# Mixture-of-experts layer behind gated power attention, one core: the overflow lists, their fetches and the first expert's outputs put elsewhere in the order

## The chip, the cores and the metric

One core of one Trainium2 chip runs the whole kernel as one program. The metric is the device time of one execution in microseconds; less is better. The program has one instruction stream for each engine: TensorE (matmuls and transposes), ScalarE, VectorE, GpSimd (which also issues all indirect transfers) and SyncE (which issues the plain transfers). They meet by semaphores alone, and each stream runs strictly in its order.

## The reference

The input is 4 sequences of 1024 tokens with 256 channels. Two sublayers follow each other, each with a residual and a layer norm behind it:

```python
x = _layernorm(x + attention(x))          # 16 query heads, 8 key heads, gated, squared scores
x = _layernorm(x + ffn(x))

# ffn: N = 4096 tokens, E = 64 experts, TOP_K = 6, F = 176, capacity C = 768 slots of an expert
scores = softmax(x @ gate_w.T); topk_w, topk_idx = top_k(scores, 6)      # weights normalised
buf[e, pos] = x[token]                                                   # the expert's slots
eo = (silu(buf @ w_gate.T) * (buf @ w_up.T)) @ w_down.T                  # for each expert
y[token] += eo[e, pos] * weight
y += shared_swiglu(x)                                                    # FS = 352, for all tokens
```

How many slots of an expert are filled depends on the data: 384 in the mean, at most 768.

## The kernel before

`schedule()` writes one list of tasks by hand, `order`. Each engine's program walks through the whole list and does its own part of every task that it knows. So a task's place in the list is its place in the queue of every engine that has a part in it. There is no planner; waits are written out in each part, and `Once` leaves out a wait that the engine has already passed.

The stages are attention (32 heads), routing (interleaved with the last heads and with the stage behind it), the shared expert, the routed experts, and a last stage that sums two partial outputs and normalises.

The shared expert is done as 16 jobs (`2 * M`, `M = 8` blocks of 512 tokens, two halves of FS each). A job is `gate_up` in 3 parts (TensorE, `gate_up`, L1286), `hidden` in 4 parts (ScalarE L1503 to L1521, VectorE L1892 to L1907), and for each block two `shared_down`. In `shared_up` (inside `schedule`) the steps of the last routing part are mixed in by `paces[k]`, up to job 10.

A routed expert is handled with its first 512 slots (`MAIN`) in a main job. Slots 512 to 767 of experts that have more than 512 tokens are handled by overflow jobs of 256 slots. `KJ = 4` of these have a fixed place in the sequence `SEQ` (places 18, 34, 50 and 67); further ones run in branches at the end. Which expert an overflow job serves is only known at run time: `counted` (L1912) counts the experts with more than 512 tokens and scans the count over the experts, `jobs` (L1927) makes from it, in four chunks of 12, the row numbers of the slots and of the weights. Both run on VectorE, in the buffers `scores` and `onehot` of routing.

For one place of `SEQ` the order is: part 0 of this job's `gate_up`; `turn` of the next job's rows (TensorE transposes 4 tiles in two pairs, `turn_x`; ScalarE makes `xe_hi`, L1530; VectorE makes `xe_lo`, L1969, and picks the token numbers and weights); `split_hi` of the weights two jobs on (ScalarE, L1501) and `split_lo` (VectorE, L1888); parts 1 and 2 of `gate_up`; and the two pairs of `down` of the job *before* (TensorE L863, ScalarE scales them into `y_e`, L1548, GpSimd adds them to `y_part` in DRAM by four indirect transfers of 128 rows each, L2117). `down` and `turn_x` share two PSUM banks in turn: each waits until the use before of its bank has been read (`out_before`). `down` also waits until VectorE has made the lower halves of the job's hidden layer (`c_hl`).

SyncE loads each expert's rows (`rows_in`, L1060) and weights (`raw_in`, L1035); there are four buffers of each. The overflow jobs' rows and weights are fetched by GpSimd: `over_in` (L2137) at place 0 does, for each of the four, two row fetches (L2125, into `acc`, a buffer that attention used) and one weight fetch (L2132, into a buffer that overlaps the shared expert's inputs, hence the wait for all of its `gate_up`, `c_gu`). Each such call waits at its head for the lists (`c_jobs`), for the routing's own scatters (`all_sent`), for the first layer norm and for `c_gu`; GpSimd's `down` parts are behind it in its queue.

Of the kernel before, what the change touches and what calls it, by code (L numbers as in the profile page):

```python
# [24 lines left out]
E, F, FS, TOPK, CAP_FACTOR = 64, 176, 352, 6, 2  # L25
# [45 lines left out]
KJ = 4  # L71
# [4 lines left out]
SEQ = list(range(E))  # L76
# [88 lines left out]
def schedule():  # L165
# [5 lines left out]
    def do(*task):  # L171
        order.append(task)
# [245 lines left out]
    def route_some(count):  # L418
        while to_send:
            do(*to_send.pop(0))  # L420
        for _ in range(min(count, len(background))):
            route_step(*background.pop(0))
            while to_send:
                do(*to_send.pop(0))

    def hidden(k):
        for part in range(4):
            do("hidden", k, part)
# [21 lines left out]
    def shared_up(m):  # L450
        for k in (2 * m, 2 * m + 1):
            if k > 3:
                for i in range(3):
                    do("gate_up", k, i)
            if k > 2:
                route_some(paces[k])
                hidden(k)


    paces = [0, 0, 0, 3, 3, 3, 3, 3, 2, 3, 2]  # L460
    assert sum(paces) == len(background)
    paces += [0] * (2 * M - len(paces))
    for m in range(M):
        if m + 1 < M:
# [13 lines left out]
            for part in range(3):  # L478
                do("split_lo", m - 2, part)
    assert not background and not to_send  # L480
    do("counted",)
    do("jobs", 0)


    def turn(x_id):
        for pair in range(tiles_of(x_id) // 2):
            on_spare("turn_x", x_id, pair)
        do("pick", x_id)
# [8 lines left out]
    for place, x_id in enumerate(SEQ):  # L497
        k = 2 * M + place
        after = SEQ[place + 1:place + 4]
        if 3 <= place < 2 + JOBS // JC:  # L500
            do("jobs", place - 2)
        if x_id + 2 < E:
            do("rows_in", x_id + 2)
        if place == 0:
            for i in range(KJ):
                do("over_in", E + i)
        if len(after) > 2 and after[2] < E:
            do("raw_in", after[2])


        do("gate_up", k, 0)
        do("hidden", k, 0)
        if after:
            turn(after[0])
        if len(after) > 1:
            do("split_hi", after[1])
        do("gate_up", k, 1)
        if len(after) > 1:
            do("split_lo", after[1], 0)
        do("hidden", k, 1)  # L520
        if len(after) > 1:
            do("split_lo", after[1], 1)
        do("gate_up", k, 2)
        do("hidden", k, 2)
        if place:
            down(SEQ[place - 1], (0,))
        do("hidden", k, 3)
        if len(after) > 1:
            do("split_lo", after[1], 2)
        if place:  # L530
            down(SEQ[place - 1], (1,))
    down(SEQ[-1], (0, 1))
    return order, spare
# [28 lines left out]
def build(nc, xT, x, wall, wvall, wg, gw, bc, wffn, table, out):  # L562
# [64 lines left out]
    with ExitStack() as ctx:  # L627
# [109 lines left out]
        xo = [half(i).rearrange("p (j c) -> p j c", c=ROW) for i in range(KJ)]  # L737
# [70 lines left out]
        c_r = [signal(f"c_r{i}") for i in range(XS)]  # L808
# [8 lines left out]
        o_moved = [signal(f"o_moved{q}") for q in range(KJ)]  # L817
# [1239 lines left out]
        def pool_program(e):  # L2057
            once = Once(e)
# [63 lines left out]
            def fetch_rows(q, x_rows, sem):  # L2122

                for t in range(OVER_TILES):
                    e.indirect_dma_start(  # L2125
                        out=x_rows[:, t, :], out_offset=None, in_=slots, in_offset=bass.IndirectOffsetOnAxis(
                            ap=job_rows[:, q, t:t + 1], axis=0),
                        bounds_check=(E + 1) * CAP - 1, oob_is_err=True).then_inc(sem, 16)
# [5 lines left out]
                        ap=job_w[:, q:q + 1], axis=0),  # L2134
                    bounds_check=NX * P - 1, oob_is_err=True).then_inc(sem, 16)

            def over_in(x_id):  # L2137
                once.wait_ge(c_jobs, 1)
                all_sent(once)
                once.wait_ge(s_x1, len(PARTS))  # L2140
                once.wait_ge(c_gu, 3 * 2 * M)
                fetch_rows(x_id - E, xo[x_id - E], o_moved[x_id - E])
                fetch_weights(x_id - E, w_raw_o[x_id - E], o_moved[x_id - E])

            def down(x_id, pair):
                part = part_of(x_id)
                once.wait_ge(*out_of(("down", x_id, pair)))
                if pair == 0:
                    for i in range(YS):
                        once.wait_ge(c_store[i], 16 * len(range(i, M, YS)))  # L2150
                    once.wait_ge(s_x1_out[0], 16 * B)
                    once.wait_ge(s_x1_out[1], 16)

                    if before_job(x_id, 2) is not None:
                        once.wait_ge(c_add[part], added(before_job(x_id, 2)))
                for j in (2 * pair, 2 * pair + 1):
                    add_rows(row_token[kept_at(x_id)][:, j:j + 1], j, PLACE[x_id] % YS, part, c_add[part])

            parts = dict(acc_add=acc_add, em_mask=em_mask, x_rest=x_rest, w_rest=w_rest, wv_rest=wv_rest, wc_rest=wc_rest, route=route, scatter=scatter, over_in=over_in,
                         experts_begin=experts_begin, down=down)  # L2160

            e.memset(ones[:, :], 1.0).then_inc(s_ones)
# [211 lines left out]
```

## Time and profile before

| | us |
|---|---|
| timed runs | 2325.22, 2325.56, 2337.62 |
| median | 2325.56 |
| profiled execution | 2336.74 |
| its span | 2334.9 |

| engine | busy us | share of the span |
|---|---|---|
| TensorE, matmuls | 2203.9 | 94% |
| VectorE | 1329.0 | 57% |
| ScalarE | 1203.6 | 52% |
| GpSimd | 818.2 | 35% |

Rows of the profile name the engines PE (TensorE), PEld (its weight loads), DVE (VectorE), ACT (ScalarE), POOL (GpSimd) and SPq (SyncE's queue). Times are microseconds from the start of the span. L1213 is line 1213 of the kernel. The shares are averages over stages: the routed experts, which the change touches, run from about 1760 to 2292 us.

### The profile page before, as it was taken

The numbers are of one execution on the slowest core, as the hardware profiler recorded it, in microseconds if no ns is written. First come the engines' busy times: TensorE is split into PE (matmuls) and PEld (weight loads), VectorE is DVE, ScalarE is ACT, GpSimd is POOL, SyncE is SP. The second block draws the span as 40 slices with busy tenths as digits, with TensorE's granted clock in tenths as the row PEclk, the third lists the DMA queues.
The fourth block names the chain that finished last, engine by engine and source line by source line (L and its number), as shares of the span: only waits on it lengthen the run. The fifth ranks groups of instructions, "written<-read, shape, count | busy, mean of one in ns | idle before, by whom it ended". The sixth has DMA issues, their size and how long they took to land.

```text
span 2334.9 us, 38657 instructions
## 1 busy us (share of the span) xinstructions
PE 2203.9 (94%) x14776; PEld 1988.5 (85%) x14776; DVE 1329.0 (57%) x2870; ACT 1203.6 (52%) x2231; POOL 818.2 (35%) x791
## 2 busy tenths in 40 slices
PE   8999999999999999999999999998888999999970
PEld 7999998998989899898988889997777888888860
DVE  3444444454655454555545475446657887878853
ACT  4544444444444454444445444444335777777753
POOL 3121112000014500002540014400445878888785
PEclk9999999999999999999999999999899999999995
DMA  4866721122113212111322213211548989888856
GB/s 173 333 255 260 302 80 60 45 61 84 50 54 119 89 57 79 52 50 59 120 86 81 64 53 101 87 61 57 188 149 269 218 198 213 198 207 204 211 62 231
DMA packets 152704, 310.60 MB, mean 133 GB/s; under 512 B 26528, under 2 KB 88224, under 8 KB 152512
## 3 DMA queue, kind: packets, MB, share of 16 engines
q1 hardware_dynamic: 103888, 251.98, 32.3%
q0 software_dynamic: 48192, 55.68, 12.3%
q8 instruction: 119, 1.95, 0.3%
q14 instruction: 73, 0.60, 0.1%
q10 hardware_dynamic: 432, 0.40, 0.1%
HBM read 168.01 MB, written 149.34 MB: 136 GB/s over the span
## 4 chain that ended last, share of the span: by engine, by line
PE 85%; DVE 5%; issue 3%; ACT 3%; POOL 2%; DMA 1%; another core or an unknown queue 0%; SPq 0%; POOLq 0%; ACTq 0%; DVEq 0%
PE bank L853 52%; PE bank L1213 20%; PE bank L863 7%; PE bank L1316 2%; PE bank L1226 2%; POOL y_part L2117 1%; DVE ub L1718 1%; DMA w_raw<-in_wall 0%; DVE stats L2032 0%; ACT q_hi L1441 0%; POOL slots L2107 0%; ACT x1t_hi L1483 0%; POOL xt_lo L2069 0%; DVE bank L1902 0%; ACT silu_b L1517 0%
## 5 line engine op out<-in xcount | busy, mean ns | idle before, releaser
L1213 PEld LDWEIGHTS bank<-v,a 128*128 128x128 f32 x4608 | 603.8, 191 | 43.9 <-ACT a L1465 0.8
L1213 PE MATMUL bank<-v,a 128*128 128x129 f32 x4608 | 617.3, 275 | 0.6 <-ACT a L1465 0.6
L2117 POOL DMA_INDIRECT y_part<-y_e,row_token x264 | 414.1, 1569 | 102.8 <-issue 87.2
L2087 POOL TENSOR_TENSOR decay_all<-decay_all,tab 128x128 f32<-128x128 f32 x128 | 60.2, 470 | 919.9 <-DMA decay_all<-decay_dram 919.5
L1461 ACT ACTIVATE a<-bank,c_s 128x512 f32<-128x512 f32 x384 | 263.4, 686 | 179.0 <-PE bank L853 164.3
L1465 ACT ACTIVATE a<-ub 128x512 f32<-128x512 f32 (+1 forms) x256 | 133.9, 524 | 377.7 <-DVE ub L1718 360.0
L2107 POOL DMA_INDIRECT slots<-rows,slot_u x192 | 189.2, 985 | 307.3 <-PE bank L1213 132.1
L853 PE MATMUL bank<-q_hi,k_hi 128*128 128x512 f32 (+1 forms) x640 | 261.7, 409 | 8.6 <-DVE ub L1718 8.0
L1697 DVE TENSOR_TENSOR q_lo<-bank,q_hi 128x512 fp32r<-128x512 f32 x128 | 88.5, 692 | 273.6 <-ACT q_hi L1441 271.0
L853 PE MATMUL bank<-q_lo,k_hi 128*128 128x512 f32 (+1 forms) x640 | 237.4, 371 | 0.0
L853 PE MATMUL bank<-q_hi,k_lo 128*128 128x512 f32 (+1 forms) x640 | 236.4, 369 | 0.0
L853 PE MATMUL bank<-xe_hi,wf_hi 128*128 128x512 f32 (+2 forms) x504 | 205.0, 407 | 11.3 <-DMA xe_lo<-x1t_dram 5.7
L853 PE MATMUL bank<-xe_lo,wf_hi 128*128 128x512 f32 (+2 forms) x504 | 198.4, 394 | 1.7 <-issue 1.6
L853 PE MATMUL bank<-xe_hi,wf_lo 128*128 128x512 f32 (+2 forms) x504 | 198.3, 393 | 0.1
L853 PE MATMUL bank<-xt_hi,w_hi 128*128 128x512 f32 x384 | 166.1, 432 | 2.4 <-DVE acc L1758 1.3
L853 PE MATMUL bank<-wc_hi,yt_hi 128*128 128x256 f32 x512 | 155.3, 303 | 2.9 <-DVE yt_lo L1748 2.9
L1758 DVE TENSOR_TENSOR acc<-bank,acc 128x512 f32<-128x512 f32 x128 | 88.1, 689 | 117.8 <-PE bank L853 116.6
L1718 DVE TENSOR_TENSOR ub<-bank,em 128x512 f32<-128x512 f32 (+1 forms) x256 | 140.8, 550 | 18.1 <-PE bank L853 8.7
L853 PE MATMUL bank<-xt_hi,w_lo 128*128 128x512 f32 x384 | 150.9, 393 | 0.0
L853 PE MATMUL bank<-xt_lo,w_hi 128*128 128x512 f32 x384 | 150.6, 392 | 0.0
L853 PE MATMUL bank<-wc_hi,yt_lo 128*128 128x256 f32 x512 | 145.5, 284 | 0.0
L853 PE MATMUL bank<-wc_lo,yt_hi 128*128 128x256 f32 x512 | 145.3, 284 | 0.0
(215 smaller groups left out, 4918.2 us busy)
## 6 DMA issues: line engine op xcount, KB each, us to landing
slots<-acc SPq DMA_DIRECT2D x65, 816.0 KB, 7.8
w_raw_f<-in_wffn SPq DMA_DIRECT2D x66, 624.0 KB
xr<-slots SPq DMA_DIRECT2D x64, 544.0 KB
decay_all<-decay_dram SPq DMA_DIRECT2D x128, 128.0 KB
w_hi<-w_dram SPq DMA_DIRECT2D x24, 384.0 KB
w_lo<-w_dram SPq DMA_DIRECT2D x24, 384.0 KB
sum<-y_part SPq DMA_DIRECT2D x16, 512.0 KB, 10.9
wc_hi<-wc_dram SPq DMA_DIRECT2D x24, 256.0 KB
```

The costliest lines, as they stand in the source:

```text
L853: ins = e.matmul(dst, a, b, start=first and i == 0, stop=last and i == len(passes) - 1, skip_group_check=True)
L863: ins = e.matmul(dst, a, b, start=first and n_ == 0 and p_ == 0, stop=n_ == len(steps) - 1 and p_ == len(passes) - 1, skip_group_check=True)
L1213: ins = e.matmul(dst[:, tt, r, :], a32[u % NA][:, r, t0:t0 + P], v[n % 3][:, s, :], start=(s == 0 and r == 0), stop=(s == 2 * g + tt), ski ...
L1226: ins = e.transpose(ps[:, r, tt * P:(tt + 1) * P], yn[j % YR][:, tt, r, :], ident)
L1461: e.activation(squares, score_bank(u)[:, 0:R * w].rearrange("p (r t) -> p r t", r=R), ACT.Square, scale=c_s[b % 2][:, g * (g - 1) + s, h:h ...
L1465: e.activation(squares, ub[masked_nth[u] % 2][:, :, 0:w], ACT.Square).then_inc(s_sq)
L1697: e.tensor_tensor(lo, bank[6 + m % 2][:, :], f32(hi), ALU.subtract).then_inc(s_out_of[m % 2])
L1718: e.tensor_tensor(ub[mine % 2][:, :, 0:w], score_bank(u)[:, 0:R * w].rearrange("p (r t) -> p r t", r=R), decay.unsqueeze(1).to_broadcast([ ...
L1758: e.tensor_tensor(part, bank[6 + m % 2][:, :].rearrange("p (t c) -> p t c", c=C), part, ALU.add).then_inc(s_out_of[m % 2])
L2087: e.tensor_tensor(arg[:, GROUP:GROUP + P], arg[:, P:GROUP], mask, ALU.add)
L2107: e.indirect_dma_start(out=slots, out_offset=bass.IndirectOffsetOnAxis(ap=slot_u[:, j, k:k + 1], axis=0), in_=rows[:, j, :], in_offset=Non ...
L2117: e.indirect_dma_start(out=y_part[part], out_offset=bass.IndirectOffsetOnAxis(ap=token, axis=0), in_=y_e[y][:, j, :], in_offset=None, boun ...
```

## The change

Three things are moved; nothing is computed otherwise.

1. `counted` and the first chunk of `jobs` stand behind the hidden layer of shared job 11, right after the last routing step, and no longer behind the whole shared expert.
2. `over_in` is cut in two. `over_rows` for all four overflow jobs comes first and waits, besides the lists, the scatters and the first layer norm, for the rows of experts 0 and 1 to have landed, but not for `c_gu`. `over_weights` for all four follows and waits for `c_gu`.
3. Both pairs of `down` of the first expert stand, at the second place, ahead of parts 1 and 2 of `gate_up` instead of behind them. From the third place on the order is as it was.

```diff
@@ in shared_up(m)
             if k > 2:
                 route_some(paces[k])
                 hidden(k)
+            if k == jobs_at:
+                do("counted",)
+                do("jobs", 0)
     paces = [0, 0, 0, 3, 3, 3, 3, 3, 2, 3, 2]
     assert sum(paces) == len(background)
+
+    jobs_at = len(paces)
     paces += [0] * (2 * M - len(paces))
...
     assert not background and not to_send
-    do("counted",)
-    do("jobs", 0)
...
         if place == 0:
-            for i in range(KJ):
-                do("over_in", E + i)
+            for what in ("over_rows", "over_weights"):
+                for i in range(KJ):
+                    do(what, E + i)
...
             do("split_hi", after[1])
+        if place == 1:
+
+            down(SEQ[0], (0, 1))
         do("gate_up", k, 1)
...
         do("hidden", k, 2)
-        if place:
+        if place > 1:
             down(SEQ[place - 1], (0,))
         do("hidden", k, 3)
         if len(after) > 1:
             do("split_lo", after[1], 2)
-        if place:
+        if place > 1:
             down(SEQ[place - 1], (1,))
...
-            def over_in(x_id):
+            def over_rows(x_id):
                 once.wait_ge(c_jobs, 1)
                 all_sent(once)
                 once.wait_ge(s_x1, len(PARTS))
+
+                for r in range(2):
+                    once.wait_ge(c_r[r], 16)
+                fetch_rows(x_id - E, xo[x_id - E], o_moved[x_id - E])
+
+            def over_weights(x_id):
+
                 once.wait_ge(c_gu, 3 * 2 * M)
-                fetch_rows(x_id - E, xo[x_id - E], o_moved[x_id - E])
                 fetch_weights(x_id - E, w_raw_o[x_id - E], o_moved[x_id - E])
```

## Rows read from the trace of the kernel before

**Rows 1.** The page, part 4: share of the chain of waits by engine.
```profile
PE 85%; DVE 5%; issue 3%; ACT 3%; POOL 2%; DMA 1%; another core or an unknown queue 0%; SPq 0%; POOLq 0%; ACTq 0%; DVEq 0%
```

**Rows 2.** GpSimd, 1781 to 2292 us: group (busy us, mean ns, idle before), then timeline (start, us).
```profile
L2117 POOL DMA_INDIRECT y_part<-y_e,row_token x264 | 414.1, 1569 | 102.8 <-issue 87.2 <-ACT y_e L1548 8.3 <-DMA y_part<-y_e,row_token 4.4
...
2289.84 1.54 POOL L2117 DMA_INDIRECT y_part<-y_e,row_token  x1 [0.30 <-issue]
```

**Rows 3.** Windows: us, busy us (instructions) by engine, PEclk, DMA share, GB/s.
```profile
2250.00:2334.00 84.00, 13.11 (x92) 11.79 (x90) 30.53 (x103) 28.37 (x63) 53.53 (x32) 0.59 0.64 178
```

**Rows 4.** Chain of waits in order of time (start us, us, what), steady part.
```profile
1816.84 2.76 PE bank L853 x12
...
1824.24 2.77 PE bank L853 x12
```

**Rows 5.** Timeline of GpSimd and ScalarE around the first adds.
```profile
1781.20 1.61 POOL L2117 DMA_INDIRECT y_part<-y_e,row_token  x1 [6.77 <-ACT y_e L1548]
...
1807.40 1.77 POOL L2117 DMA_INDIRECT y_part<-y_e,row_token  x1 [2.75 <-issue]
...
1815.53 1.54 POOL L2117 DMA_INDIRECT y_part<-y_e,row_token  x1 [0.68 <-issue]
...
1813.95 0.82 ACT L1548 ACTIVATE y_e<-bank,row_w 128x256 f32<-128x256 f32 x2
```

**Rows 6.** Timeline of VectorE around the lists and their new place.
```profile
1722.21 0.68 DVE L1907 TENSOR_TENSOR hb<-bank,hb 48x512 fp32r<-48x512 f32 x1
1730.52 0.70 DVE L1899 TENSOR_TENSOR bank<-bank,silu_a 128x512 f32<-128x512 f32 x1 [7.63 <-ACT silu_a L1510]
...
1752.82 0.20 DVE L1915 TENSOR_SCALAR scores<-taken 128x64 f32<-128x64 f32 x1
...
1757.46 0.17 DVE L1943 CAST job_w<-job_w_f 128x12 uint32<-128x12 f32 x1
1760.74 0.69 DVE L1969 TENSOR_TENSOR xe_lo<-bank,xe_hi 128x512 fp32r<-128x512 f32 x1 [3.11 <-ACT xe_hi L1530]
```

**Rows 7.** Windows with a lower granted clock (PEclk is third from the end).
```profile
1718.00:1735.00 17.00, 11.88 (x32) 7.39 (x32) 6.24 (x10) 6.17 (x12) 10.16 (x11) 0.70 0.35 120
...
1776.00:1780.00 4.00, 4.00 (x22) 3.69 (x22) 3.03 (x8) 2.73 (x6) 0.00 (x0) 0.66 1.02 398
```

**Rows 8.** GpSimd's first and last fetch of twelve, SyncE's first row loads, a window.
```profile
1758.46 1.07 POOL L2125 DMA_INDIRECT acc<-slots,job_rows  x1 [17.91 <-DVE job_w L1943]
...
1773.41 1.01 POOL L2132 DMA_INDIRECT w_raw_o<-in_wffn,job_w  x1 [0.30 <-issue]
...
1743.53 1.49 SPq L1060 DMA_DIRECT2D xr<-slots  x2
...
1750.00:1758.40 8.40, 8.40 (x72) 8.40 (x72) 6.54 (x23) 2.98 (x5) 0.00 (x0) 1.00 0.19 63
```

**Rows 9.** DMA queues from 1764 to 1774 us: packets, MB, share of 16 engines.
```profile
q1 hardware_dynamic: 520, 2.20, 54.8%
q0 software_dynamic: 438, 1.74, 45.6%
```

**Rows 10.** Timeline of TensorE and VectorE at the second expert.
```profile
1770.15 1.09 PE L1316 MATMUL bank<-tab,xr 128*128 128x128 f32 x8 [1.10 <-DMA xr<-slots]
...
1775.62 0.36 PE L863 MATMUL bank<-wf_hi,ha_hi 128*128 128x256 f32 x1 [1.60 <-issue]
...
1773.35 0.69 DVE L1907 TENSOR_TENSOR hb<-bank,hb 48x512 fp32r<-48x512 f32 x1
...
1774.79 0.69 DVE L1969 TENSOR_TENSOR xe_lo<-bank,xe_hi 128x512 fp32r<-128x512 f32 x1
```

**Rows 11.** Chain of waits, 1750 to 1800 us: its shares, then pieces.
```profile
by line: PE bank L863 19.2%; issue 15.7%; ACT xe_hi L1530 6.5%; another core or an unknown queue 5.5%; DVE bank L1899 5.5%; ACT wf_hi L1501 4.8%; DVE xe_lo L1969 4.8%; ACT silu_b L1517 4.7%; DVE bank L1902 4.2%; DVE job_x L1934 3.9%; DVE wf
...
1749.99 9.60 PE bank L863 x80
...
1765.62 1.00 issue
```

More of the change, by code:

```diff
@@ L2157, in down @@
                     add_rows(row_token[kept_at(x_id)][:, j:j + 1], j, PLACE[x_id] % YS, part, c_add[part])
-            parts = dict(acc_add=acc_add, em_mask=em_mask, x_rest=x_rest, w_rest=w_rest, wv_rest=wv_rest, wc_rest=wc_rest, route=route, scatter=scatter, over_in=over_in,
+            parts = dict(acc_add=acc_add, em_mask=em_mask, x_rest=x_rest, w_rest=w_rest, wv_rest=wv_rest, wc_rest=wc_rest, route=route, scatter=scatter, over_rows=over_rows, over_weights=over_weights,
                          experts_begin=experts_begin, down=down)
```

## The prediction

> **What bounds the kernel now.** I read the page first. The chain of waits lies on TensorE for 85% of the span [rows 1]. That is an average over two stages, so I read the second one, where the change is, by itself. From 1781.20 us to 2291.38 us GpSimd issues the 264 indirect adds of the experts' outputs. They take 1569 ns each in the mean and are mostly 0.30 us apart [rows 2]: 264 x (1.569 + 0.30) = 493 us of the 510.2 us between the first and the last. From 2250 us to the end TensorE is busy for only 13.11 us [rows 3], while the adds run to 2291.38 us; behind the last add come its landing, the transfers in of both halves of the output and the last sums. So GpSimd's queue ends the stage. TensorE keeps almost the same pace: its list of waits is empty from 1822 to 2250 us, and its pieces for one expert start again after 7.40 us (1816.84 to 1824.24 us) [rows 4]. Four adds are 4 x 1.845 = 7.38 us. The two lie within a few hundredths of a microsecond, and GpSimd ends last because it also slips now and then.
>
> The question is therefore when GpSimd's adds get into their unbroken row. They start at 1781.20 us but are broken: ahead of the fourth expert's adds by 2.75 us and ahead of the fifth's by 0.68 us, where 0.30 us are the rule [rows 5]; the third's are broken too. From the sixth on only the 0.30 us stand between them, apart from late slips. In front of the fifth expert's adds GpSimd was waiting for its data: ScalarE's copy of them ended at about 1814.77 us (start 1813.95 us and 0.82 us) [rows 5], 0.76 us ahead of the add. So the end of the kernel hangs on how early TensorE, VectorE and ScalarE bring the *fifth* expert's outputs, not the first's. An earlier first add only makes the first breaks longer.
>
> **The change part by part.**
>
> *Lists made earlier.* The list work of VectorE (the count, the scan and one chunk of jobs) starts at 1752.82 us and ends at 1757.63 us: 4.81 us [rows 6]. VectorE's next operation is at 1760.74 us and waits for ScalarE, which waits for TensorE's last shared products. So taking it away from there gives nothing: it had 3.11 us of cover left [rows 6]. Its new place is behind the hidden layer of shared job 11, whose last operation ends at 1722.89 us; the next is at 1730.52 us after 7.63 us idle [rows 6]. 4.81 us fit in, with 2.8 us to spare. Cost 0. Were that gap closed (it comes from a slow stretch of TensorE, clock 0.70 over 1718 to 1735 us [rows 7]), the lists would cost up to 4.81 us. The chunks for the fourth to sixth expert stay where they are.
>
> *Rows fetched earlier.* GpSimd's twelve fetches (8 of rows, 4 of weights) start at 1758.46 us, 1.32 us apart, and the last ends at 1774.42 us [rows 8]. The new waits in front of the eight row fetches are for the lists (now early) and for the rows of experts 0 and 1. These two transfers are issued from 1743.53 us, and from 1750 us on the DMA engines are nearly idle (share 0.19 over 8.4 us) [rows 8]; so I put the start at 1750 us. Eight fetches by 1.32 us end at 1760.6 us. The weights' own wait, for all shared gate and up products (over at 1749.99 us, when the last shared outputs' 80 matmuls start [rows 11]), is by then past, and four by 1.32 us end at 1765.9 us, 8.5 us earlier. Behind the waiting instruction on GpSimd stand only these fetches and the adds, and the first add waits for its data until 1781.20 us [rows 5]: its idle time of 6.77 us only grows. On the DMA engines 1.1 MB (8 x 128 rows of 1088 bytes) leave a crowded stretch for an idle one. The four weight transfers start sooner, though (first at about 1760.6 in place of 1761.2 us, last at 1764.6 in place of 1773.4 us), exactly when SyncE's loads of experts 2 to 5 begin. At 1764 to 1774 us the engines are full and the two queues share them as 54.8% and 45.6% [rows 9]. Since GpSimd's queue has a backlog in both kernels there, SyncE's loads see nearly the same share. What hangs on them: ScalarE's split of expert 2's weights (1.00 us wait at 1765.62 us) [rows 11] and TensorE's turn of expert 2's rows (1.10 us) [rows 10]. I bound this from below by those waits going, -1.0 us, and from above by the row of one weight's own copy being displaced: 0.64 MB at the (2.20 + 1.74) MB in 10 us of that stretch is 1.6 us. I take 0, near both.
>
> The Trainium skill ("DMA: Bandwidth & Descriptors", Queues, rings and completion order) says that each DMA engine takes turns between the queues for which it has work, packet by packet; the shares above agree. By that rule the weights cannot starve SyncE's loads but can halve them for as long as they last, which is what the 0 assumes.
>
> *First outputs put forward.* This is the term that counts. At the second expert TensorE's order was: 6 matmuls, turn of expert 2 (1770.15 us), 12 matmuls (from 1770.99 us), then the products of the first expert's outputs, at 1775.62 us after a wait of 1.60 us [rows 10]. What they wait for: VectorE's last split of the first expert's hidden layer (1773.35 + 0.69 = 1774.04 us) and the PSUM bank, free when VectorE has split expert 2's turned rows (1774.79 + 0.69 = 1775.48 us) [rows 10]. None of these hangs on the 12 matmuls. In the new order the outputs stand *before* the 12 matmuls. They cannot start earlier than 1775.5 us, so TensorE is idle from 1771.2 us on and the 12 matmuls, until now under the wait, come behind: 2.76 us (the row of 12 in the chain) [rows 4]. Then everything follows: the third expert's first products start at about 1781.8 in place of 1779 us (1775.6 us, 2.4 us for 20 matmuls by the row of 80 in 9.60 us [rows 11], and about 1 us of lower clock), its turn and ScalarE's and VectorE's splits go with it. The chain of waits runs in that stretch over TensorE's transposes, ScalarE's and VectorE's splits, and then over VectorE's list chunks (3.9% on the reduction of one of them alone) [rows 11]; so it passes the 2.8 us on to the fifth expert's outputs. The first outputs themselves come earlier: 10 of the 80 matmuls, 1.2 us, from 1775.6 us, ScalarE's 0.82 us and the 0.76 us up to the add give 1778.4 us in place of 1781.20 us for GpSimd's first add, 2.8 us early; then it stands idle longer before experts 2 to 5.
>
> Bounds of this term. From below: the chain of 1750 to 1800 us holds 5.5% of "another core or an unknown queue" [rows 11], 2.75 us of waits of ScalarE that are no work; if they all vanish, the bank is free at 1775.5 - 2.8 = 1772.7 us, and of the 12 matmuls' 2.76 us some 1.5 us still stand behind (1772.7 - 1771.2). From above: TensorE is idle for 4.3 in place of 1.6 us, and the granted clock already falls to 0.66 over 1776 to 1780 us after that shorter idle time [rows 7], its lower level of 1.2 GHz for most of the stretch. With the 17 us at 0.70 as the nearest row of a long fall [rows 7], 17 x 0.30 = 5.1 us of work would be lost; so up to +7.9 us. I take +2.8.
>
> The Trainium skill ("TensorE: Matmul & The Clock Gate", Part 1: The HAM clock gate) says that an array which has been idle is given the 1.2 GHz clock; the trace agrees, with 0.66 behind the idle 1.6 us. It speaks against this part of the change and is a rival below.
>
> *Sum.* 0 + 0 + 2.8 us: the span goes from 2334.9 to 2337.7 us. The profiled execution took 2336.74 us, 1.8 us around its span, so 2339.5 us. It lies 11.2 us above the median: the three timed runs are 2325.22, 2325.56 and 2337.62 us, two levels 12 us apart. I add the term to the median: 2325.56 + 2.8 = 2328.4 us. What a measurement of this kernel can tell from no change is about 0.5%, 11.6 us; the forecast is within it.
>
> **The rivals.**
> - *The adds' start decides* (chance 0.16). If GpSimd's queue were the bound from the first add on, the 2.8 us by which it starts earlier would be the gain: 2322.8 us. For it: TensorE is nearly done at 2250 us and the adds are not [rows 2, 3]. Against it: the breaks up to the fifth expert [rows 5].
> - *Absorbed* (0.25). The 2.8 us are made up: by the transfers landing earlier (-1.0 and the 1.10 us of the turn), or by a later slip of GpSimd's queue that would have come anyway. 2325.6 us. For it: GpSimd's row holds 510.2 - 493 = 17 us beyond adds and issue, of which the early breaks are some 4; the rest looks accidental. Against it: TensorE, which follows the same pace, has no idle time from 1822 us on.
> - *The idle array loses its clock* (0.11), the case clearly on the slow side. The 4.3 us of TensorE idle at 1771 us, with the crowding of four weight transfers in one piece, bring a longer stretch at 1.2 GHz: 2.8 + 5.1 = +7.9 us, 2333.5 us. It decides if over some 4 us of extra low clock follow 1776 us.
> - *The other level* (0.12). The median of the new runs lies at the upper of the two levels: 2328.4 + 12 = 2340.4 us, with the mechanism as forecast.
> - *It does not do what it says* (0.04). If the rows of expert 1 land late, GpSimd fetches as late as before, and only the order on TensorE is left: 2328.4 us.
>
> **How the numbers follow.** The forecast, 2328.4 us, has 0.32. For 8 in 10 the range leaves out about one on each side: from 2318 us (the early-start case and a few microseconds of lucky slips) to 2342 us (the upper level). Faster by over 0.5% needs -11.6 us, which no case gives: 0.05 for what I have not seen. Slower by over 0.5% needs +11.6 us: the level, 0.12, and a part of the clock case, together 0.14. Within 0.5%: 0.81.
>
> **What would show it.** VectorE's lists at about 1723 to 1728 us, with no later hidden layer delayed. GpSimd's row fetches from about 1750 us, the weights' last end at about 1766 us. TensorE's idle time ahead of the first outputs grows from 1.6 to about 4.3 us and the 12 matmuls start at about 1779 us. The first add starts at 1778 to 1779 us, but the breaks ahead of the second to fifth experts' adds grow by some 5.6 us in sum, and the fifth expert's first add is at about 1818.3 in place of 1815.53 us; the last one as much later. I am wrong if the fifth expert's add comes as early as before or earlier, or if the first outputs start well before 1775 us because VectorE and ScalarE are done sooner in a less crowded DMA.

## The result, and the profile after

| | us |
|---|---|
| kernel before, median of 22 runs | 2331.86 (2321.0 to 2337.62) |
| kernel after, median of 22 runs | 2341.43 (2332.54 to 2348.03) |
| ratio after / before | 1.0042, 95% interval [1.0031, 1.0052] |
| profiled execution after (before) | 2342.93 (2336.74) |
| its span (before) | 2341.1 (2334.9) |

The changed kernel is slower by 0.42%, within the 0.5% of the forecast's middle class and 9.6 us by the medians, where 2.8 us were forecast. The 22 runs of before also fill the range from 2321 to 2338 us without a gap: there are no two levels 12 us apart, as three runs had suggested. One run of e4 below took 2785.49 us at a granted clock of 0.745; e4's time is given without it.

First the page of the kernel after: TensorE's busy time, the chain of waits by engine, and the group of adds. They answer to [rows 1, 2]; none of them tells of a change.

```profile
PE 2205.5 (94%) x14776; PEld 1988.3 (85%) x14776; DVE 1328.9 (57%) x2870; ACT 1203.9 (51%) x2231; POOL 819.9 (35%) x791
...
PE 86%; DVE 5%; issue 3%; ACT 3%; POOL 2%; DMA 1%; another core or an unknown queue 0%; ACTq 0%; POOLq 0%; SPq 0%; DVEq 0%
...
L2124 POOL DMA_INDIRECT y_part<-y_e,row_token x264 | 415.6, 1574 | 118.6 <-issue 84.3
```

VectorE's timeline of the kernel after (start, us, instruction, idle time before it and its releaser), against [rows 6]: the lists stand from 1722.19 to 1726.99 us, and the next job's operation waits for ScalarE as it did before.

```profile
1722.19 0.20 DVE L1922 TENSOR_SCALAR scores<-taken 128x64 f32<-128x64 f32 x1
...
1726.82 0.17 DVE L1950 CAST job_w<-job_w_f 128x12 uint32<-128x12 f32 x1
1729.50 0.70 DVE L1906 TENSOR_TENSOR bank<-bank,silu_a 128x512 f32<-128x512 f32 x1 [2.52 <-ACT silu_a L1517]
```

GpSimd's timeline after, against [rows 5, 8]: the last scatter of routing, the first and the last of the twelve fetches, and the first add of experts 1, 2, 4 and 5.

```profile
1738.17 0.97 POOL L2114 DMA_INDIRECT slots<-rows,slot_u  x1 [0.30 <-issue]
1749.26 1.07 POOL L2132 DMA_INDIRECT acc<-slots,job_rows  x1 [10.12 <-DMA xr<-slots]
...
1763.79 1.00 POOL L2139 DMA_INDIRECT w_raw_o<-in_wffn,job_w  x1 [0.30 <-issue]
1784.92 1.61 POOL L2124 DMA_INDIRECT y_part<-y_e,row_token  x1 [20.12 <-ACT y_e L1555]
...
1795.90 1.54 POOL L2124 DMA_INDIRECT y_part<-y_e,row_token  x1 [3.72 <-ACT y_e L1555]
...
1815.10 1.77 POOL L2124 DMA_INDIRECT y_part<-y_e,row_token  x1 [2.75 <-issue]
...
1823.22 1.54 POOL L2124 DMA_INDIRECT y_part<-y_e,row_token  x1 [0.68 <-issue]
```

The fetches stand where the forecast put them (from 1750 us, last end 1765.9 us; found 1749.26 and 1764.79 us). But the first add comes at 1784.92 us, not at 1778 to 1779, and the fifth expert's at 1823.22 us against 1815.53 before: +7.7 us. The last add ends at 2299.01 against 2291.38 us: +7.6 us. So in these two executions all of the loss is there at the fifth expert; their spans differ by 6.2 us, the medians by 9.6 us.

Where it comes from is in ScalarE's copies of the shared expert's last outputs, ahead of any routed expert. First the timeline of before, two of its four last copies, 2.40 us apart:

```profile
1757.22 0.60 ACT L1539 ACTIVATE y_e<-bank 128x512 f32<-128x512 f32 x1 [1.80 <-PE bank L863]
1759.62 0.60 ACT L1539 ACTIVATE y_e<-bank 128x512 f32<-128x512 f32 x1 [1.80 <-PE bank L863]
```

The same four in the kernel after:

```profile
1751.67 0.60 ACT L1546 ACTIVATE y_e<-bank 128x512 f32<-128x512 f32 x1 [0.44 <-PE bank L870]
1754.24 0.60 ACT L1546 ACTIVATE y_e<-bank 128x512 f32<-128x512 f32 x1 [1.97 <-PE bank L870]
1759.28 0.60 ACT L1546 ACTIVATE y_e<-bank 128x512 f32<-128x512 f32 x1 [4.44 <-PE bank L870]
1766.41 0.60 ACT L1546 ACTIVATE y_e<-bank 128x512 f32<-128x512 f32 x1 [6.53 <-remote]
```

The first is 0.75 us earlier than before (1752.42 us there), the last 6.79 us later. The chain of waits of the kernel after over 1750 to 1800 us names no engine for its second longest piece, the wait of 6.51 us:

```profile
1749.96 9.30 PE bank L870 x74
1759.28 0.60 ACT y_e L1546
1759.88 6.51 another core or an unknown queue
1766.41 0.61 ACT y_e L1546
1767.02 0.04 issue
1767.06 1.13 PE bank L1323 x4
```

TensorE had dispatched the 80 matmuls of these outputs without a pause from 1749.08 to 1758.83 us, as before. Yet ScalarE was released only at about 1766.4 us. In the trace's semaphore events (an increment is what a semaphore counts as one signal) TensorE's increment for the last copy, due at 1758.83 us, is at 1766.39 us, 7.6 us late. The one for the four transposes behind it, which end at 1760.65 us, is at 1766.45 us, 0.06 us later. These four transposes take over 0.6 us, so they can't have been done between the two events; the work was done, and its signals came late together. The last fetch of GpSimd ends at 1764.79 us, 1.6 us before. VectorE's and ScalarE's signals are not held up: from 1600 to 1800 us none of VectorE's 145 and of ScalarE's 92 increments in the kernel after is over 1 us late.

The windows (us, busy us and instructions by engine PE, PEld, DVE, ACT, POOL, then granted clock, DMA share, GB/s) show the same stretch of both kernels, before first: TensorE busy for 5.8 us less under the same DMA load.

```profile
1758.40:1774.50 16.10, 12.86 (x70) 9.90 (x69) 7.60 (x17) 7.11 (x12) 12.61 (x12) 1.00 0.87 316
```

```profile
1758.40:1774.50 16.10, 7.08 (x29) 5.50 (x28) 2.18 (x6) 3.80 (x7) 5.03 (x5) 0.68 0.87 316
...
1776.00:1780.00 4.00, 3.18 (x18) 2.42 (x16) 3.29 (x6) 2.05 (x5) 0.00 (x0) 1.00 1.02 416
...
1781.00:1790.00 9.00, 8.21 (x49) 7.20 (x50) 5.34 (x12) 5.45 (x11) 4.47 (x3) 1.00 0.72 198
```

### The profile page after: what moved, and what is told of

Its sections match the earlier page's. It is cut to its first block, busy times and chain, and to the rows that moved or that the text cites. A ratio compares the mean times of both kernels' runs of the same rounds, so it can differ in the third digit from the quotient of the medians.

```text
span 2341.1 us, 38657 instructions
## 1 busy us (share of the span) xinstructions
PE 2205.5 (94%) x14776; PEld 1988.3 (85%) x14776; DVE 1328.9 (57%) x2870; ACT 1203.9 (51%) x2231; POOL 819.9 (35%) x791
## 4 chain that ended last, share of the span: by engine, by line
PE 86%; DVE 5%; issue 3%; ACT 3%; POOL 2%; DMA 1%; another core or an unknown queue 0%; ACTq 0%; POOLq 0%; SPq 0%; DVEq 0%
PE bank L860 53%; PE bank L1220 20%; PE bank L870 8%; PE bank L1323 2%; PE bank L1233 2%; POOL y_part L2124 1%; DVE ub L1725 1%; DVE stats L2039 0%; ACT q_hi L1448 0%; POOL slots L2114 0%; DVE bank L1909 0%; ACT x1t_hi L1490 0%; POOL xt_lo L2076 0%; ACT silu_b L1524 0%
```

## The experiments

Theory A: while GpSimd issues indirect transfers without a break (1.28 to 1.32 us from start to start), TensorE's semaphore increments arrive late; the change moved twelve of them over the last shared outputs. Theory B: the new order of the first outputs is what costs. Theory C: it is the transfers' traffic, not their issuing (the expectations of e1, e3 and e4 have a narrower form of it: four weight transfers in one piece hold up SyncE's loads).

Each ratio is to the kernel before on the same chip (its medians there: 2334.1 us for e1 to e4, 2332.83 for e5 to e8, 2334.07 for e9 to e12). "Last copy" is the start of the last shared output's copy by ScalarE, "fifth add" that of the fifth expert's first add, each in the one profiled execution. What stands ahead of the last copies moves them too: the first of the four starts at 1747.36 us in e1 and at 1753.03 us in e4. So how late they are is better read from the first to the last of the four: 7.20 us in most executions with the signals on time.

| kernel | median us | ratio to before | last copy | fifth add |
|---|---|---|---|---|
| before | 2331.86 to 2334.1 | 1 | 1759.62 | 1815.53 |
| after | 2341.43 | 1.0042 [1.0031, 1.0052] | 1766.41 | 1823.22 |
| e1 order back | 2338.2 | 1.0015 [1.0, 1.003] | 1760.97 | 1817.04 |
| e2 order only | 2336.29 | 1.001 [0.9992, 1.0028] | 1758.22 | 1820.47 |
| e4 lists only | 2337.43 | 1.0017 [1.0002, 1.0032] | 1768.86 | 1823.22 |
| e3 spaced fetches | 2334.14 | 0.9994 [0.9978, 1.001] | 1753.99 | 1812.25 |
| e5 spaced, order back | 2329.93 | 0.999 [0.9974, 1.0005] | 1757.83 | 1813.37 |
| e7 spaced less | 2328.96 | 0.9972 [0.9958, 0.9986] | 1755.87 | 1809.26 |
| e8 plain fetches | 2335.45 | 1.0006 [0.9994, 1.0018] | 1759.65 | 1815.84 |
| e6 scatters spaced | 2318.38 | 0.9932 [0.9912, 0.9952] | 1752.37 | 1805.44 |
| e10 scatters only | 2324.26 | 0.9953 [0.9934, 0.9973] | 1750.13 | 1807.13 |
| e11 third spaced | 2331.53 | 0.9987 [0.9974, 1.0] | 1755.33 | 1808.00 |
| e12 narrow both | 2325.39 | 0.996 [0.9944, 0.9976] | 1753.43 | 1806.64 |
| e9 both spaced | 2317.46 | 0.9924 [0.9905, 0.9943] | 1745.78 | 1800.69 |

### One part of the change at a time: e1, e2, e4

e1 is the kernel after with the outputs in the old order:

```diff
-        if place == 1:
-            down(SEQ[0], (0, 1))
-        if place > 1:
+        if place:
             down(SEQ[place - 1], (0,))
```

> The changed kernel with the first expert's outputs put back behind the gate and up products; lists and row fetches stay early. Theory A (the loss comes from where GpSimd's unbroken run of 12 indirect fetches lies: while it lasts, TensorE's semaphore signals reach the other engines late, and it now lies over the last shared outputs, where every engine waits for just these signals): the last shared output's copy by ScalarE is still some 6 us late, the time stays 5 to 9 us above the kernel before. Theory B (my forecast's term: the order on TensorE costs 2.8 us and more through the clock): the loss goes, within 2 us of before. Theory C (four weight transfers in one piece hold up SyncE's loads): the loss stays, but with SyncE's loads landing late and not the copy.

e2 is the kernel before with that edit alone, the other way round.

> The kernel before with only the first expert's outputs put forward; lists late and fetches as before. Theory A: no change of place of the fetches, so only the order's own cost: 0 to +3 us. Theory B: +2.8 to +9 us, the whole loss. Theory C: 0.

e4 is the kernel before with the lists made early; its fetches stay in one `over_in`, and start at 1751.53 us since their lists are there.

```diff
+            if k == jobs_at:
+                do("counted",)
+                do("jobs", 0)
...
-    do("counted",)
-    do("jobs", 0)
```

> The kernel before with only the lists made early. The fetches (rows and weights mixed, in the old order) can then start when the last shared gate and up product is done, at about 1750 us instead of 1758 us. Theory A: the run of 12 fetches lies over the last shared outputs, as in the changed kernel: ScalarE's copies of the last two blocks' outputs are late by 3 to 7 us, and the time is 4 to 9 us above before. Theory B: no change. Theory C: about half of the changed kernel's loss, since three of the four weight transfers are then under way before SyncE's loads start.

The early fetches bring the late copies with them whatever the order: e1's last two copies wait 3.47 and 6.54 us for an unnamed releaser, and e4's wait 5.65 and 6.59 us. From the first to the last of the four copies there are 14.74 us in the kernel after, 13.61 us in e1 and 15.84 us in e4, against 7.20 us in the kernel before and in e2. ScalarE's timeline of e4:

```profile
1755.43 0.60 ACT L1541 ACTIVATE y_e<-bank 128x512 f32<-128x512 f32 x1 [1.80 <-PE bank L865]
1761.68 0.60 ACT L1541 ACTIVATE y_e<-bank 128x512 f32<-128x512 f32 x1 [5.65 <-PE bank L865]
1768.86 0.60 ACT L1541 ACTIVATE y_e<-bank 128x512 f32<-128x512 f32 x1 [6.59 <-remote]
```

In e2 the fetches start at 1757.06 us and the copies are on time. What is late there is TensorE at the first outputs (TensorE's timeline of e2):

```profile
1776.30 0.55 PE L866 MATMUL bank<-wf_hi,ha_hi 128*128 128x256 f32 x1 [6.20 <-DVE xe_lo L1972]
...
1777.30 0.41 PE L866 MATMUL bank<-wf_lo,hb 112*128 112x256 f32 x1
1777.51 0.41 PE L866 MATMUL bank<-wf_hi,ha_hi 128*128 128x256 f32 x1
```

From the last shared copy to the fifth add e2 takes 62.25 us where before takes 55.91 us. Most of that is no cost of the order by itself. TensorE's eight transposes end at 1770.11 us, and the increment of the last of them comes at 1774.44 us, 1.8 us behind the end of the run of fetches and 4.3 us late. In the kernel before the same increment is just as late (due at 1771.24, found at 1775.57 us), but TensorE had its 12 matmuls to do meanwhile.

By the medians e1 is 4.1 us and e4 3.3 us above the kernel before, less than the 5 to 9 and 4 to 9 us that theory A expected. e2's 2.2 us are not clear of no change (its interval holds 1). e4's time would fit theory C as well (about half of the loss); its late copies do not.

### The issuing or the traffic: e3, e5, e7, e8, e11

e3 is the kernel after with a memset of 1088 columns (1.02 us) on GpSimd ahead of each fetch; e5 is e3 with the old order; e7 is e5 with 544 columns (0.57 us); e11 is e5 with the memset ahead of every third fetch alone.

```diff
+            def pad():
+                once.wait_ge(s_x1_out[0], 16 * B)
+                once.wait_ge(s_x1_out[1], 16)
+                once.wait_ge(s_pad, len(pads))
+                e.memset(rows[:, 0:4, :], 0.0).then_inc(s_pad)
+                pads.append(1)
...
+                    if sem is not o_rest:
+                        pad()
```

> The changed kernel with a memset of 1088 columns on GpSimd ahead of each of the 12 indirect fetches, so that they start some 2.4 us apart instead of 1.32 and run from 1749 to about 1778 us, still ahead of the first add. Theory A in the form that the density of indirect transfers holds the signals up: the copies of the last shared outputs are on time, and the time is that of the kernel before or up to 3 us below. If any GpSimd work between them does the same harm, or if it is the number of transfers and not their density, the copies are late as before. Theories B and C: the loss stays (B), or shrinks by half (C).

> The spaced kernel (a memset of 1088 columns ahead of each of the 12 fetches) with the first expert's outputs back in their old place. With no held-up signals in either, the difference to the spaced kernel is the order's cost alone. Theory A with the order's term of my forecast: from the last shared output's copy to the fifth expert's first add 58.3 us in the spaced kernel become 55.5 us or less, and the time is 2 to 4 us below the spaced kernel and 3 to 5 us below the kernel before. If the order costs nothing, 58 us stay.

> As the kernel e5 with half the memset (544 columns, some 0.55 us), so the fetches start about 1.9 us apart, nearly the 1.85 us of the adds, which hold up nothing. If density decides with a bound between 1.32 and 1.85 us, the last shared outputs' copies are on time (2.40 us apart) and the time is that of e5. If the bound lies higher, they are late by some us.

> The changed kernel with the outputs in the old order and a memset of 1088 columns ahead of every third fetch only: four runs of three fetches, each run some 3.9 us long. Theory A1 (the run must be long; a pause lets all signals through): the last four shared copies are late by under 1.5 us each, the fifth expert's first add comes within 56.5 us of the last shared copy, ratio 0.998 to 1.000. Theory A2 (any two fetches 1.3 us apart hold signals up for as long as they are issued): each run of three holds a signal up to 3 to 4 us, copies late by 2 to 4 us, ratio 1.000 to 1.002.

GpSimd's timeline of e3: the fetches are 2.2 us apart and lie over the same last outputs as in the kernel after.

```profile
1746.85 1.07 POOL L2145 DMA_INDIRECT acc<-slots,job_rows  x1 [0.16 <-issue]
1747.92 1.03 POOL L2137 MEMSET rows<- 128x1088 f32 x1
1749.11 1.03 POOL L2145 DMA_INDIRECT acc<-slots,job_rows  x1 [0.17 <-issue]
```

ScalarE's last copies in e3 are 2.40 us apart again, with the same waits of 1.80 us as before:

```profile
1751.59 0.60 ACT L1547 ACTIVATE y_e<-bank 128x512 f32<-128x512 f32 x1 [1.80 <-PE bank L871]
1753.99 0.60 ACT L1547 ACTIVATE y_e<-bank 128x512 f32<-128x512 f32 x1 [1.80 <-issue]
```

The same holds in e5, in e7 (fetches 1.75 us apart) and in e11 (runs of three fetches 1.32 us apart, with one longer step of 2.2 us between runs). e11 had been made to tell a pause from a density: its copies are on time and no increment of TensorE over the fetches is more than 1 us late. So in this execution runs of three do no harm, and one pause in some five microseconds is enough.

e3 differs from the kernel after by the spacing alone, and its ratio is 0.9994 in place of 1.0042: 0.5%, all of the loss. In the old order (e1 against e5) it is 1.0015 to 0.999. Two expectations were off: e5 is 0.04% under e3 by the ratios, about 1 us, where 2 to 4 us were expected, and e7, expected at e5's time, is 0.18% under it. The intervals of e5 and e7 overlap, and no cause of that difference is shown.

e8 moves the twelve transfers from GpSimd to SyncE, as plain transfers of the same size. It leaves out the choice of experts: the overflow jobs always get the rows and weights of experts 0 to 3.

```diff
+            def over_rows(x_id):
+                ...
+                for t in range(OVER_TILES):
+                    e.dma_start(xo[q][:, t, :], slots[q * CAP + MAIN + t * P:q * CAP + MAIN + (t + 1) * P, :]).then_inc(o_moved[q], 16)
+            def over_weights(x_id):
+                ...
+                e.dma_start(w_raw_o[q][:, :], wffn[q]).then_inc(o_moved[q], 16)
```

> The changed kernel, outputs in the old order, with the 12 indirect fetches replaced by 12 plain transfers of the same sizes that SyncE issues at the same point (about 1750 us, behind the rows of experts 0 and 1); it leaves out the choice of experts, the overflow jobs get the rows and weights of experts 0 to 3. This keeps the traffic and takes away GpSimd's issuing. Theory A (GpSimd's issuing holds the signals up): the last shared outputs' copies are on time, 2.40 us apart. If the traffic of the weights beside the last shared outputs does it, they are late as in the changed kernel, by 2 to 7 us.

GpSimd's timeline of e8 has nothing between the last scatter and the first add, and ScalarE's last copy is on time, at 1759.65 us behind 1.80 us of waiting:

```profile
1739.76 0.97 POOL L2124 DMA_INDIRECT slots<-rows,slot_u  x1 [0.30 <-issue]
1780.93 1.58 POOL L2134 DMA_INDIRECT y_part<-y_e,row_token  x1 [40.20 <-ACT y_e L1565]
```

The bytes are the same and the DMA engines are busier over the last outputs (share 0.82 over 1750 to 1758.4 us, 0.54 in the kernel after), yet the late signals are gone: theory C falls. What e8 does not tell apart is the issuing on GpSimd from the queue that it fills: the indirect fetches go through `q0 software_dynamic`, e8's through `q1 hardware_dynamic`. e8 gains nothing on the whole (1.0006), and why is not shown: SyncE's loads for expert 2 begin at 1760.75 us, as before (1760.71 us), but the DMA share over 1758.4 to 1774.5 us is 1.02 in place of 0.87.

Over all profiled executions the count is plain. From 1745 to 1800 us the six kernels whose fetches run unbroken (before, after, e1, e2, e4, e10) have 5, 2, 4, 4, 3 and 5 increments of TensorE that are over 1 us late; the eight others have none.

### The same thing in the routing: e6, e10, e12, e9

The kernel before has its own unbroken runs: the last 48 scatters of routing, 1.28 us apart, over 1652 to 1741 us. There too increments of TensorE come up to 10.7 us late (10.9 us in e8). e10 is the kernel before with nothing but a short memset ahead of each of them:

```diff
+        space = sb(ctx, "space", [P, 256])
...
+                    if PARTS[p][0] == B - 1:
+                        once.wait_ge(s_space, len(spaces))
+                        e.memset(space[:, :], 0.0).then_inc(s_space)
+                        spaces.append(1)
```

e6 is e5 with this edit, e12 is e7 with it, and e9 is e7 with it at 512 columns.

> As e5, and a memset of 256 columns ahead of each of the 48 routing scatters of the last sequence too, which now run 1.28 us apart in runs of 8 to 16; TensorE's signals are late by up to 10 us at the end of three such runs in every trace so far. Theory A: with the scatters some 1.7 us apart these late signals go, and with them the slow clock behind them: the stage ends 5 to 10 us earlier, unless the scatters' own end, 20 us later by the memsets, holds up the rows of the first experts: then it ends as late or later. Under theories B and C nothing of this happens and the kernel is slower by the later rows.

> The kernel before with nothing but a memset of 256 columns ahead of each of the last 48 routing scatters. Theory A: the gain of the spaced scatters does not need the moved lists or fetches. It is the gain of e6 (0.68%) less that of the spaced fetches alone (0.1 to 0.3%): ratio 0.994 to 0.997, and TensorE is busy for some 4 us more of 1600 to 1760 us than before. Rival (the gain in e6 came from the spaced fetches meeting an earlier first add): ratio 0.999 to 1.001.

> The same as e9_both_spaced, but with 256 columns ahead of the scatters, as in e6, and 544 ahead of the fetches, as in e7. Theory A: the gains add, e6's with 5 us fewer of fetches: the last fetch ends some 5 us earlier than in e6, ratio 0.991 to 0.994; it is level with or up to 4 us behind e9 if wider gaps between the scatters free more signals, and up to 8 us ahead of it if e9's scatters end too late.

> The changed kernel with the outputs in the old order, a memset of 544 columns ahead of each of the twelve fetches and one of 512 columns ahead of each of the last 48 routing scatters (some 0.5 us between scatters where 256 columns gave 0.17). Theory A (GpSimd's unbroken run of indirect transfers holds TensorE's signals up, the denser the more): no signal of TensorE is late by more than 1 us from 1650 us on, the shared copies start 2.40 us apart, and the time is 14 to 20 us under the kernel before (ratio 0.991 to 0.994). Rival: it is enough to have some gap, and the wider one only makes the last scatters end later (about +10 us against the narrow gap if the queue has no slack), so rows of experts 0 and 1 land late and the ratio comes back to 0.995 to 1.0.

GpSimd's timeline of e9 shows the scatters 1.68 us apart and the fetches 1.80 us apart:

```profile
1738.47 0.97 POOL L2119 DMA_INDIRECT slots<-rows,slot_u  x1 [0.16 <-issue]
1739.44 0.55 POOL L2117 MEMSET space<- 128x512 f32 x1
1740.15 0.97 POOL L2119 DMA_INDIRECT slots<-rows,slot_u  x1 [0.16 <-issue]
...
1749.09 1.07 POOL L2149 DMA_INDIRECT acc<-slots,job_rows  x1 [0.24 <-issue]
1750.16 0.56 POOL L2141 MEMSET rows<- 128x544 f32 x1
1750.89 1.03 POOL L2149 DMA_INDIRECT acc<-slots,job_rows  x1 [0.17 <-issue]
```

The groups of ScalarE's shared copies over 1600 to 1760 us (busy, mean ns, idle before them by releaser), before and e9. The idle time with an unnamed releaser, 11.7 us, is gone:

```profile
L1539 ACT ACTIVATE y_e<-bank 128x512 f32<-128x512 f32 x16 | 9.0, 593 | 20.9 <-remote 11.7 <-PE bank L863 9.2
```

```profile
L1545 ACT ACTIVATE y_e<-bank 128x512 f32<-128x512 f32 x16 | 8.7, 583 | 5.0 <-PE bank L869 3.6 <-issue 1.4
```

And the window over the same stretch, before and e9: 5.3 us more of work of TensorE in it, at a higher granted clock (0.97 in place of 0.91).

```profile
1600.00:1760.00 160.00, 139.55 (x803) 118.15 (x802) 99.58 (x213) 61.05 (x103) 50.90 (x55) 0.91 0.40 137
```

```profile
1600.00:1760.00 160.00, 144.85 (x859) 124.69 (x859) 109.32 (x230) 66.03 (x114) 87.24 (x115) 0.97 0.49 166
```

The count of increments of TensorE that came over 1 us late between 1600 and 1800 us, and the latest, from the trace's semaphore events (each against the end of the last instruction that carries it, so at least that late):

```
kernel    apart, us (scatters / fetches)   late over 1 us   latest by, us
before    1.28 / 1.32                      12 of 119        10.7
after     1.28 / 1.32                       8 of 117        10.7
e11       1.28 / runs of three              9 of 123        10.2
e10       1.46 / 1.32                      23 of 126         4.6
e6        1.46 / 2.2                       13 of 126         9.0
e12       1.46 / 1.75                      14 of 122         7.9
e9        1.68 / 1.75                       0 of 114         none
```

From 1800 to 2280 us, where GpSimd's adds stand 1.84 us apart, not one in these kernels is late by over 1 us. With 256 columns (e10) more increments are late than in the kernel before, 23 in place of 12, but none by over 4.6 us, and the kernel is 0.47% faster; so the few long waits seem to cost more than the many short ones. e6's expectation that its late signals would go was wrong, 13 of 126 are left, while its gain of 14.5 us is more than the 5 to 10 us expected.

e9 is the fastest version: 16.6 us under the kernel before by the medians (ratio 0.9924 [0.9905, 0.9943]), with no work removed and 60 memsets added. Its shared job 12 starts on ScalarE at 1717.06 us in place of 1729.82, its last copy is 13.8 us earlier, its fifth add 14.8, its last add 16.7. e10's gain alone (0.47%) answers the rival in its expectation: the scatters' gain needs nothing of the change. e12 missed its expectation: 0.996 lies outside the 0.991 to 0.994, 8 us behind e9 where at most 4 were expected. The wider gap (0.70 in place of 0.48 us from the end of one scatter to the start of the next) seems to be worth more than I gave it: with 256 columns increments are still up to 7.9 us late. The profiles do not show the 8 us, since e12's profiled execution is its fastest (2318.84 us) and level with e9's (2318.55 us). That e6, the same but for slower fetches, has 0.9932 is not explained; the two intervals just overlap.

## Why the prediction came out as it did

**The class and the sign were right, the size was not, and the failed step is "Rows fetched earlier", whose cost was put at 0.** That 2341.43 us lies inside the range was luck: the upper end of 2342 us stood there for a level that does not exist, and what brought the time near it was on no list of rivals. By the forecast's own steps:

*What bounds the kernel.* It held: a delay at the fifth expert's adds is passed on to the end. From its first add to the end of the last one there are 475.85 us before, 475.79 us after, 473.4 to 476.0 us in the other kernels but one (e12: 468.6 us). Whether GpSimd's adds or TensorE, which keeps the same pace, sets this distance no run tells, and e12 shows that it can be shorter. After's first add is 3.7 us late, its fifth expert's 7.7, its last 7.6.

*Lists made earlier, cost 0.* Right, with their gap: 2.52 us of VectorE's idle time are left behind them. But e4 (ratio 1.0017 [1.0002, 1.0032]) shows that this part alone does harm, through what it lets GpSimd start.

*Rows fetched earlier, cost 0.* The place was right to 1.1 us, and so was the cover of GpSimd's own queue (idle ahead of the first add for 20.12 us). The step failed in what it left out: it priced the fetches by GpSimd's queue and by the DMA engines, and took TensorE's last shared outputs, over which they now stand, as untouched. They cost 6.79 us at the last shared copy, nearly all of the 7.7 us. SyncE's store of these outputs waits for the same copy, so its loads for expert 2 begin at 1767.50 us, in place of 1760.71 us. In the kernel before the same twelve fetches stand 9 us later, over stretches in which fewer waits hang on TensorE's signals, and cost less: there ScalarE shows waits of 1.54, 0.46 and 0.83 us with an unnamed releaser.

The sign of it stood in the rows. The forecast read the 5.5% of "another core or an unknown queue" [rows 11] as waits that are no work and that might vanish, and used them for the lower bound. A kernel on one core has no other core. What runs in these moments is GpSimd's fetches (1758.46 to 1774.42 us). The group of shared copies above, with its 11.7 us of the same kind over the scatters, would have hinted at the mechanism and its price (up to 6.77 us for a wait) before the change.

*First outputs put forward, +2.8 us.* The mechanism was right: TensorE's timeline of the kernel after shows it idle for 2.62 us (about 4.3 us were forecast) ahead of the first outputs, behind the next expert's transposes, with the 12 matmuls of the first products now behind them:

```profile
1778.14 1.04 PE L1323 MATMUL bank<-tab,xr 128*128 128x128 f32 x8
1781.80 0.36 PE L870 MATMUL bank<-wf_hi,ha_hi 128*128 128x256 f32 x1 [2.62 <-DVE xe_lo L1976]
```

With the fetches spaced (e3 against e5) the way from the last shared copy to the fifth add is 58.26 us in the new order and 55.54 us in the old: +2.72 us. That this is so close to the forecast is in part chance: three more kernels in the old order and with no late signal over their fetches, e6, e7 and e11, have 53.08, 53.40 and 52.67 us. With late signals about, the same edit costs 0.74 us (after against e1) or 6.34 us (e2 against before), according to what they hit.

The medians divide the loss otherwise than this pair of profiles. Between e1 and after, the order, lie 0.27%, some 6 us; between before and e1, the early fetches in the old order, 0.15%, some 4 us, each good to some 3 to 5 us. So how much of the 9.6 us each part has is not settled. What both ways of reading agree on is that the loss needs the late signals: in e3 both parts are there, the signals over the fetches are on time, and nothing is lost (0.9994 [0.9978, 1.001]).

*The clock rival* (0.11) did not decide: behind the 2.62 us, which end at 1781.80 us, the granted clock is 1.00 over 1781 to 1790 us. It is 1.00 over 1776 to 1780 us too (the windows above), where it was 0.66 in [rows 7]. The low clock, 0.68 over 1758.4 to 1774.5 us, follows the 6.5 us of late signals. In e2, behind 6.20 us idle, the matmuls start 0.21 us apart in place of 0.12 and the granted clock is 0.50 over 1776 to 1781 us, its level of 1.2 GHz: there the rival did take place. By my estimate it is some 2 us of e2's 6.3: 21 matmuls at 0.09 us more each. The Trainium skill ("TensorE: Matmul & The Clock Gate", Part 1: The HAM clock gate) says that an array that has been idle is given 1.2 GHz; e2 agrees with it, while behind the 2.62 us in the kernel after the clock was 1.00.

*The other level* (0.12) named 2340.4 us, close to what came, for a reason that does not exist: the runs do not have two levels. *Absorbed* and *the adds' start decides* fell by the fifth add. The base was too low as well: the median of 22 runs is 6.3 us above that of three.

The sum as the two profiles give it: lists 0, fetches over the last outputs +6.8, order +0.7 (forecast +2.8; the rest hides behind the late signals): 7.5 us, against 7.7 us found at the fifth add and 9.6 us between the medians.

## What to carry to other kernels

When queued work is moved into a gap of its engine, ask which *other* engines run there and whose signals are awaited, not only whether the queue and the DMA engines have room: twelve fetches that fitted their gap to a microsecond kept ScalarE from its last copy for 6.8 us, in the execution that was profiled. On one core a wait for "another core or an unknown queue" or "remote" is a finding, not noise: lay it beside every other engine's timeline. And where GpSimd issues dozens of indirect transfers while TensorE feeds others through semaphores, try some 0.7 us between them: with it (and with the lists made early) this kernel is 0.76% faster.

## What the runs showed of the hardware

- While GpSimd issues indirect transfers without a pause (scatters 0.98 us with 0.30 us between, fetches 1.01 us with 0.30), TensorE's semaphore increments can arrive up to 10.7 us late (10.9 us in e8, over its scatters), often several at once. Most of them come 0.6 to 2.7 us behind the run's end, some within the run (e1: at 1760.95 us, 1.1 us before its end). TensorE goes on dispatching meanwhile; who waits for it stands still. VectorE's and ScalarE's increments are not late in the kernels before and after.
- At starts 1.46 us apart it still happens, at 1.68 us and above not once in the profiled executions; runs of three 1.32 us apart (e11, one execution) delay none, and neither do the adds, 1.54 us with 0.30 us between.
- The same bytes as plain transfers of SyncE do not do it (e8). So it goes with the transfers that GpSimd issues and with their pace, not with the bytes; whether with the issuing itself or with the queue that it fills is open.
- What inside the chip holds the increments up stays open: a path shared by GpSimd's descriptors and TensorE's increments would fit, but no run looks there. Open too is whether the spread of the kernel before from run to run (17 us) is made by it. e9's six timed runs spread by 5.4 us, e10's ten by 16.3 us, which would fit, but six are few, and e8, with increments up to 10.9 us late, spreads by 8.1 us over twelve.
